# A fused attention and expert block: routing per sequence by ranks and mostly on GpSimd, and a new order of steps

## The reference

```python
def _L0_xattn_ref(image_features, text_features, Wq, bq, Wk, bk, Wv, bv):
    query = einsum('bqi,ih->bqh', image_features, Wq) + bq      # key, value from text_features
    scores = einsum('bqh,bkh->bqk', query, key) * scale
    return einsum('bqk,bkh->bqh', softmax(scores), value)

def _L0_ffn_ref(X, ...):                                        # 16 heads of 8, 8 experts, top 2
    h = rmsnorm(X, norm1_w)
    q, k, v = (h @ w for w in (wq, wk, wv))
    X = X + (softmax(q k^T * scale) v) @ wo
    h2 = rmsnorm(X, norm2_w)
    probs = softmax(h2 @ router_w)
    topw, topi = top_k(probs, 2);  topw = softmax(topw)
    combine = sum(one_hot(topi) * topw)
    shared = swiglu(h2, sh_gate, sh_up, sh_down)
    spec = sum over the 8 experts of combine[:, e] * swiglu(h2, e_gate[e], e_up[e], e_down[e])
    return X + shared + spec

x = x + tanh(g_xattn[0]) * _L0_xattn_ref(_layernorm(x), ctx_768, ...)
x = x + tanh(g_ffn[0]) * _L0_ffn_ref(_layernorm(x), ...)
```

## Time and profile before

| What | Value |
|---|---|
| median of 3 runs | 221.45 us (220.26 to 221.53) |
| profiled execution, device time | 220.48 us |
| its span, first to last instruction | 218.6 us |
| mean granted clock of TensorE | 0.984 |
| busy: PE, DVE, ACT, POOL | 193.9, 139.4, 106.8, 54.6 us |

### The profile page before, as it was taken

One profiled execution on the slowest core, in us unless ns is written; L12 is line 12 of the kernel. 1 busy time (PEld: TensorE's weight loads), 2 busy tenths in 40 slices (PEclk: granted clock), 3 DMA queues, 4 the chain that ended last, 5 costly groups with the idle time before them and its releaser, 6 DMA issues.

```text
span 218.6 us, 4395 instructions
## 1 busy us (share of the span) xinstructions
PE 193.9 (89%) x1575; PEld 167.1 (76%) x1575; DVE 139.4 (64%) x357; ACT 106.8 (49%) x215; POOL 54.6 (25%) x88
## 2 busy tenths in 40 slices
PE   7388995997888979879898989988999999999994
PEld 5265764874866757657686859978999999999993
DVE  2604667789596766857774765889665564554653
ACT  2636374665477757958788734324222223223220
POOL 2917396122010075216841034300000000000000
PEclk9959999999999999999999999999999999999999
DMA  5941993055457935793200000000000000000000
GB/s 139 234 128 22 160 163 42 17 69 69 69 70 94 139 108 70 86 132 103 78 0 0 3 0 0 3 0 1 17 10 3 0 25 3 0 3 24 0 4 24
DMA packets 8998, 11.55 MB, mean 53 GB/s; under 512 B 976, under 2 KB 6992, under 8 KB 8752
## 3 DMA queue, kind: packets, MB, share of 16 engines
q1 hardware_dynamic: 8976, 11.27, 29.1%
HBM read 5.50 MB, written 0.52 MB: 28 GB/s over the span
## 4 chain that ended last, share of the span: by engine, by line
PE 76%; DVE 14%; ACT 4%; issue 3%; POOL 1%; DVEq 0%; POOLq 0%; ACTq 0%
PE bank L1117 14%; PE bank L1106 7%; PE bank L1105 7%; PE bank L1107 7%; PE bank L1088 7%; PE bank L1062 6%; PE bank L1073 5%; DVE mxs L849 4%; PE bank L939 4%; PE bank L954 3%; PE bank L1126 2%; PE bank L930 2%; ACT k_st L519 2%; PE bank L1010 1%; PE bank L946 1%
## 5 line engine op out<-in xcount | busy, mean ns | idle before, releaser
L849 DVE TENSOR_REDUCE mxs<-bank 128x2 f32<-128x512 f32 x64 | 41.4, 687 | 15.2 <-PE bank L1062 14.8
L637 ACT ACTIVATE ep<-bank 128x512 f32<-128x512 f32 x64 | 36.5, 605 | 14.1 <-PE bank L1073 13.6
L1105 PE MATMUL bank<-split,whi 128*128 128x256 f32 x144 | 43.2, 300 | 0.0
L1106 PE MATMUL bank<-split,whi 128*128 128x256 f32 x144 | 40.7, 283 | 0.0
L1107 PE MATMUL bank<-split,wlo 128*128 128x256 f32 x144 | 40.2, 279 | 0.0
L1117 PE MATMUL bank<-down_s,early 128*128 128x128 f32 x288 | 38.3, 276 | 2.1 <-DVE early L866 2.0
L657 ACT ACTIVATE early<-bank 128x512 f32<-128x512 f32 x28 | 16.7, 598 | 46.9 <-PE bank L1107 46.9
L1117 PEld LDWEIGHTS bank<-down_s,early 128*128 128x128 f32 x288 | 35.0, 191 | 2.6 <-DVE early L866 2.2
L869 DVE TENSOR_TENSOR early<-early,bank 128x512 f32<-128x512 f32 x28 | 19.3, 688 | 25.4 <-PE bank L1107 25.3
L1062 PE MATMUL bank<-k_st,q_st 80*128 80x256 f32 x128 | 29.7, 317 | 0.9 <-DVE mxs L849 0.5
L1105 PEld LDWEIGHTS bank<-split,whi 128*128 128x128 f32 x144 | 27.3, 190 | 0.0
(11 more groups left out here) (141 smaller groups left out, 274.2 us busy)
## 6 DMA issues: line engine op xcount, KB each, us to landing
raw<-expert_w SPq DMA_DIRECT2D x9, 256.0 KB, 8.2
k_st<-k_st SPq DMA_DIRECT2D x7, 256.0 KB, 5.8
q_st<-split SPq DMA_DIRECT2D x24, 64.0 KB
k_st<-split SPq DMA_DIRECT2D x24, 64.0 KB
down_s<-expert_w SPq DMA_DIRECT2D x9, 128.0 KB, 8.0
early<-ctx_T SPq DMA_DIRECT2D x1, 672.0 KB, 9.3
xs<-x_tiles SPq DMA_DIRECT2D x2, 256.0 KB, 4.8
out_dram<-x SPq DMA_DIRECT2D x4, 128.0 KB, 1.8
```

The source lines that it names most:

```text
L637: nc.scalar.activation(ep[:, n % NEP].rearrange("p t s -> p (t s)"), b_of(("exp", n))[:], ACT.Exp, scale=SCALE_H).then_inc(free(("exp", n) ...
L849: nc.vector.tensor_reduce(mxs[:, half % 2, :, 64 + h:65 + h], b_of(("max", n))[:].rearrange("p (t s) -> p t s", t=TB), AX_X, ALU.max).then ...
L1105: pe.matmul(bank, whi[:, fs], h2hi[:, hs], start=True, stop=False)
L1106: pe.matmul(bank, whi[:, fs], h2lo[:, hs], start=False, stop=False)
```

## The change

- **Routing.** It is done sequence by sequence. DVE subtracts the largest logit, and compares each logit with each other (128 x 128 results, greater and equal). POOL adds these up to a rank (0 is the largest, ties go to the lower index), and makes the two one-hot tables, the sums, the reciprocals (as powers of -1) and the weights `cw`. Per sequence: 4 instructions on DVE, 7 + 12 + 6 on POOL, 2 on ACT.
- **Moved to POOL.** y = the second layer norm's result (step y, `layer_norm`), the addition of the context to x1 (`add_context`), and the spreading of a half's maxima over 4 rows groups (`spread_maxima`): ACT now writes one group of 256 columns per half, and POOL copies it to the three others. PE waits for that copy (`m_spread`) at every head whose number is 2 modulo 8.
- **Picks.** `copy_picks` is cut in two steps, r0 and r1, which stand further back in ACT's list.
- **Items** go sequence by sequence. DVE waits for `x_ready` and, but for the shared expert, `cw_ready` of the sequence before it adds.
- **Order.** All tables of steps are new. 22 items are placed by i0 (behind slots 56, 60, 70, 71, 75, 79, 80, 81, 101, ...), where 8 were (behind slots 74, 75, 100, ...). k2 moves from slot 12 to 8, m1 and m2 from 11 and 14 to 16 and 25.

```diff
-FIRST_STEPS = """f0 g0 xn0 f1 t0 f2 q0 s0 g1 s1 p0 xn1 z0 g2 xn2 p1 q1 o0 o1 s2 s3 f3 q2 p2 j0 p3 n0 s4 o2 h0 o3
-                 p4 k0 n1 g3 e0 xn3""".split()
+FIRST_STEPS = """f0 f1 g0 f2 xn0 q0 g1 s0 t0 s1 g2 p0 p1 f3 z0 r0 o0 xn1 xn2 o1 q1 s2 s3 y0 j0 q2 p2 g3 p3 n0 r1
+                 h0 o2 s4 o3 k0 n1 p4 e0 h1 w0""".split()
...
-    dense = [(0, 0), (0, 1)] + [(e, b) for b in range(2) for e in range(1, NEXP)]
-    dense += [(e, b) for b in range(2, NB) for e in range(NEXP)]
+    dense = [(e, b) for b in range(NB) for e in range(NEXP)]
...
+            def layer_norm(b):
+                for i in range(b * TB, (b + 1) * TB):
+                    last = nc.gpsimd.tensor_scalar(y[:, i, :], x1[:, i, :], mv[:, 1, i, 0:1], small[:, 5, i:i + 1],
+                                                   ALU.subtract, ALU.mult)
+                last.then_inc(y_ready, 1)
+                pool.wait_ge(y_ready, b + 1)
+
+            def add_context(b):
+                ts = slice(b * TB, (b + 1) * TB)
+                xb, yb = (t[:, ts, :].rearrange("p t d -> p (t d)") for t in (x1, y))
+                hb = xs[:, ts, :].rearrange("p t d -> p (t d)")
+                step(nc.gpsimd.tensor_tensor(hb, yb, tg[:, 1:2].broadcast_to([P, TB * D]), ALU.mult))
+                nc.gpsimd.tensor_tensor(xb, xb, hb, ALU.add).then_inc(x_ready, 1)
+                pool.wait_ge(x_ready, b + 1)
...
+                if kind == "router":
+
+                    pool.wait_ge(rank_in, b + 1)
+                    step(nc.gpsimd.tensor_tensor(alike[:], alike[:], front[:].unsqueeze(1).broadcast_to([P, TB, NE, NE]),
+                                                 ALU.mult))
+                    step(nc.gpsimd.tensor_tensor(more[:], more[:], alike[:], ALU.add))
+                    step(nc.gpsimd.tensor_tensor(alike[:, :, :, 0:4], more[:, :, :, 0:4], more[:, :, :, 4:8], ALU.add))
+                    step(nc.gpsimd.tensor_tensor(more[:, :, :, 0:2], alike[:, :, :, 0:2], alike[:, :, :, 2:4], ALU.add))
+                    nc.gpsimd.tensor_tensor(rank.unsqueeze(3), more[:, :, :, 0:1], more[:, :, :, 1:2],
+                                            ALU.add).then_inc(rank_out, 1)
+                    pool.wait_ge(rank_out, b + 1)
+                    step(nc.gpsimd.tensor_scalar(oh1, rank, 0.0, None, ALU.is_equal))
+                    step(nc.gpsimd.tensor_scalar(oh2, rank, 1.0, None, ALU.is_equal))
...
+                if kind == "route_weights":
+                    pool.wait_ge(route_exp, 2 * b + 2)
+                    step(nc.gpsimd.tensor_tensor(rs[:, 9, ts], rs[:, 7, ts], neg_one, ALU.subtract))
+                    step(nc.gpsimd.tensor_tensor(rs[:, 8, ts], rs[:, 9, ts], neg_one, ALU.pow))
...
+            def spread_maxima(b, half):
+                is_read(pool, ("mT", b, half))
+                rows = q_st[NROW:NSEL, b % NSTACK]
+                nc.gpsimd.tensor_copy(rows[:, 4 * half + 1:4 * half + 4, :],
+                                      rows[:, 4 * half:4 * half + 1, :].broadcast_to([NH, NG // 2 - 1, L])
+                                      ).then_inc(m_spread, 1)
+                pool.wait_ge(m_spread, 2 * b + half + 1)
...
-                    rows = b_of(use)[64:NSEL, 0:L].unsqueeze(1).broadcast_to([NH, NG // 2, L])
-                    nc.scalar.mul(q_st[64:NSEL, b % NSTACK, 4 * half:4 * half + 4, :], rows, -1.0).then_inc(free(use), 1)
+                    nc.scalar.mul(q_st[NROW:NSEL, b % NSTACK, 4 * half, :], b_of(use)[NROW:NSEL, 0:L], -1.0
+                                  ).then_inc(free(use), 1)
...
-                for k, dst, signal in ((6, xs, hs_ready), (5, y, y_ready)):
-                    for i in range(b * TB, (b + 1) * TB):
...
-                    xb = x1[:, ts, :].rearrange("p t d -> p (t d)")
-                    step(nc.vector.scalar_tensor_tensor(out=xb, in0=yb, scalar=tg[:, 1:2], in1=xb,
-                                                        op0=ALU.mult, op1=ALU.add))
...
+                    step(nc.vector.tensor_reduce(rs[:, 0, ts], lg, AX_X, ALU.max))
+                    d1 = rt[:, 0, ts, :]
+                    nc.vector.tensor_tensor(d1, lg, rs[:, 0, ts].unsqueeze(2).broadcast_to([P, TB, NE]),
+                                            ALU.subtract).then_inc(free(("router", b)), 1)
+                    is_read(dve, ("router", b))
+                    mine, other = d1.unsqueeze(3).broadcast_to(square), d1.unsqueeze(2).broadcast_to(square)
+                    nc.vector.tensor_tensor(more[:], other, mine, ALU.is_gt)
+                    nc.vector.tensor_tensor(alike[:], other, mine, ALU.is_equal).then_inc(rank_in, 1)
...
+                dve.wait_ge(x_ready, b + 1)
+                if e:
+                    dve.wait_ge(cw_ready, b + 1)
...
+                    if h % 8 == 2:
+                        pe.wait_ge(m_spread, 2 * b + h // 8 + 1)
```

More of the change, by code:

```diff
@@ L89, in flamingo_block @@
     NG = NH // 2
-    NSEL = 64 + NH
-    groups = [range(0, 2), range(2, NB)]
+    NROW = 64
+    NSEL = NROW + NH
     def step_of(text):
@@ L256, in flamingo_block @@
         xn_ready, hs_ready, hi_ready, y_ready = sem("xn_ready"), sem("hs_ready"), sem("hi_ready"), sem("y_ready")
+        x_ready, m_spread, cw_ready = sem("x_ready"), sem("m_spread"), sem("cw_ready")
+        rank_in, rank_out = sem("rank_in"), sem("rank_out")
         nb_ready = sem("nb_ready")
@@ L370, in _ @@
             nc.gpsimd.memset(router_pad[:], 0.0).then_inc(pool_step, 1)
-            for i in range(NE):
-                last = nc.gpsimd.memset(widx[:, i:i + 1], float(NE - i))
-            last.then_inc(pool_step, 1)
+            nc.gpsimd.memset(neg_one, -1.0).then_inc(pool_step, 1)
+            pool.wait_ge(pool_step, done[0] + 2)
             done[0] += 2
@@ L468, in tables @@
                 pool.wait_ge(ld_ffn, 16)
+                step(nc.gpsimd.memset(front[:], 0.0))
+                for i in range(1, NE):
+                    last = nc.gpsimd.memset(front[:, i, 0:i], 1.0)
+                step(last)
                 nc.gpsimd.tensor_copy(router_pad[:, 0:NE], router_s).then_inc(router_ready, 1)
@@ L482, in _ @@
                     norm2(i // TB)
+                elif stage == "y":
+                    layer_norm(i)
                 elif stage == "z":
@@ L500, in _ @@
                             scale_h2(b)
+                            add_context(b)
+                        if kind in ("router", "route_top", "route_weights"):
+                            route(kind, b)
+                        if kind in ("mT0", "mT1"):
+                            spread_maxima(b, int(kind[2]))
                         if kind == "h2T":
@@ L513, in _, with copy_picks @@
             nc.scalar.mul(Wqk_s[:], b_of(("fold", 0))[:, 0:KD], SCALE_X).then_inc(free(("fold", 0)), 1)
-            def copy_picks(s):
-                picks = ident[64:NSEL, 64:64 + NH].rearrange("r (g p) -> r p g", p=2)
-                for p in range(2):
-                    nc.scalar.copy(k_st[64:NSEL, s, p * NG:(p + 1) * NG, :],
-                                   picks[:, p].unsqueeze(2).broadcast_to([NH, NG, L])).then_inc(picks_ready, 1)
+            def copy_picks(p):
+                picks = ident[64:64 + NH, 64:64 + NH].rearrange("r (g p) -> r p g", p=2)
+                nc.scalar.copy(k_st[64:64 + NH, 0, p * NG:(p + 1) * NG, :],
+                               picks[:, p].unsqueeze(2).broadcast_to([NH, NG, L])).then_inc(picks_ready, 1)
             act.wait_ge(ident_ready, 1)
-            copy_picks(0)
             def xn_turned(b):
@@ L671, in _ @@
                     h_turned(i)
+                elif stage == "r":
+                    copy_picks(i)
                 elif stage == "e":
@@ L731, in second_norm @@
                 dve.wait_ge(norm2_out, b + 1)
-                for k, dst, signal in ((6, xs, hs_ready), (5, y, y_ready)):
-                    for i in range(b * TB, (b + 1) * TB):
-                        last = nc.vector.scalar_tensor_tensor(out=dst[:, i, :], in0=x1[:, i, :], scalar=mv[:, 1, i, 0:1],
-                                                              in1=small[:, k, i:i + 1].broadcast_to([P, D]),
-                                                              op0=ALU.subtract, op1=ALU.mult)
-                    last.then_inc(signal, 1)
+                for i in range(b * TB, (b + 1) * TB):
+                    last = nc.vector.scalar_tensor_tensor(out=xs[:, i, :], in0=x1[:, i, :], scalar=mv[:, 1, i, 0:1],
+                                                          in1=small[:, 6, i:i + 1].broadcast_to([P, D]),
+                                                          op0=ALU.subtract, op1=ALU.mult)
+                last.then_inc(hs_ready, 1)
             def x_max(i):
```

100 lines of the change are left out of this document (42 added, 58 removed), and 27 rows, old and new, of tables (MIXED_STEPS, SEQ_STEPS).

## The result

The changed kernel takes 223.29 us (median of 11 runs, 220.85 to 227.07) against 220.67 us for the kernel before on the same chips: ratio 1.0119, 95% interval 1.0082 to 1.0156. The forecast was 213.7, in a range of 208.5 to 219.5. The profiled execution took 221.48 us, its span is 219.7.

A forecast was written before the change was run, and what follows sets the result against it. PE was taken to bound the kernel, with about 42 us of holes ahead of 149.4, and the DMA chain to set slot 48. 3.8 + 4.0 = 7.8 us off 220.48 gives 212.7, plus 1.0 for the median: 213.7, range 208.5 to 219.5.

The forecast's parts named there:

- The start: Up to slot 0: late picks save 3.7 us, the clock 2.8, y on POOL costs 1.2; 5.3 us earlier.
- From slot 0 to slot 48: The DMA chain sets this stretch, DVE and ACT savings do not count; slot 48 comes 3.8 us earlier, at 94.2.
- the term for the pads: Ahead of slot 48: pads copied later make the stacks' transfers queue, costing 1.5 us of lead (0 to 3.5).
- port contention: POOL holds two-input DVE instructions behind slot 0: DVE loses 14 us, PE perhaps 5; 218.5; chance 0.09, including POOL stalls.
- Behind slot 48: From slot 48 to the end, 120.5 us before: three holes can close, less shifted PE work; 4.0 us gained.
- (2): Behind slot 48: PE's wait for L866, DVE's 15 small routing instructions between two items, goes; 2.1 us gained.
- The 0.9 us of shifted work: About 0.9 us of PE work moves from ahead of slot 48 to behind it, a loss there.
- (3): Tail of sequence 3: of PE's waits of about 1.9 us, 0.3 is gained.
- (1): Ahead of the last heads: five items begin there instead of two, filling 2.5 of PE's 5.4 us to spare.
- POOL: POOL's additions, priced from its nearest rows, raise it from 54.6 to about 101 us, hidden; 0 lost, up to 1.5.
- The slower rival: Behind slot 48: POOL's small instructions at 0.726 us each make PE stand, some 12 us lost; 225; chance 0.05.

The follow-up runs named there:

- the splits apart: Changed kernel with GpSimd's splits of experts 0 and 1 moved (slot 5 to 3, slot 16 to 14), not directly behind second-norm powers: 213.32 us, ratio 0.9694.

## Why the prediction was wrong

*The start* held: 5.6 us of lead at slot 0 against 5.3 forecast, ACT's picks gone from the first tile, clock 1.00 from 10.6 to 17.4.

*From slot 0 to slot 48* is the step that failed. I said that the DMA chain sets this stretch, so that nothing else in it counts, and gave slot 48 a lead of 3.8 us. Measured, it came 0.85 us late. The chain only sets it as long as PE keeps up. PE was held for 2.35 and 2.56 us and then ran at half clock for two stretches of 6.9 us. The runs price that at 9.4 us: 3.1 for the waits, 6.3 for the clock (1.6 of these behind slot 48, see below). With the splits apart, slot 48 lies 60.6 us behind slot 0 (61.3 before) at 91.6, a lead of 6.5 us. So the term for the pads, 1.5 us, was not needed either. From the first DMA of stack 1 to slot 48 it was 56.5 us (35.14 to 91.59), as before, but the DMA share is 0.00 from 90 to 92 us: the DMAs were done at least 1.6 us ahead, and the chain did not set slot 48 there either.

The rival "port contention" had the mechanism, its row (1.371 us) and the rule of the Trainium skill, and still came out at 218.5 with 0.09 for its whole case. It failed in two ways. I spread 14 us of holds evenly over DVE and let a third reach PE. Of the 16 instructions that I placed behind slot 0, four of xs stand ahead of it (20.8 to 29.5 us), and the eight comparisons were not held (281 to 292 ns). The four that are left were all held, by 3.0 us together, and all of it reached PE. The order of POOL's list decides instead: m0 moved from slot 1 to slot 5 (which my list of changes did not name) and m1 from 11 to 16, right behind the two powers that release xs, with DVE and PE both waiting at that moment. The new list laid beside the trace would have shown the danger. And I counted a wait of PE at its own length. The kernel before had shown in the earlier trace rows that PE's standing still costs clock afterwards; I used that for a gain and not for a loss. The evidence against, that the eight steps of y showed no hold, said only that no split met them.

*Behind slot 48* I counted 4.0 us; the changed kernel took 120.8 us there against 120.5. With the splits apart it took 119.2, so 1.3 gained. By its terms: (2) the wait for L866 went, 2.1 us, right. The 0.9 us of shifted work, right: ten small matmuls more stand there (23, 6 and 6 at L1061, L1069 and L1054, against 16, 4 and 5 of their kind before), an estimate of 1.0 us at the 0.1 us from one to the next in a group of L1061. (3) 0.3: nothing. (1) 2.5 us of filled holes: nothing. From slot 48 to the last head's scores it takes 34.1 us for 314 matmuls, against 26.8 for 248. The 66 more cost 7.3 us, where an item's pitch (2.31 us for 20) makes them 7.6. So the holes are nearly what they were. The items do fill some, but those that the change itself makes: without them PE waits for POOL's h and for the spread, and 7.1 us are lost, the slow clock among it. The remaining 1.6 us of the changed kernel fit the slow stretch at 148.0 to 151.4, 3.4 us at half clock. It comes in some kernels and not in others with the same waits of 0.8 and 0.7 us ahead of it; why stays open.

*POOL* was priced well in sum: y 0.88 us each (0.609 forecast, too low), the spread 0.82 (0.85), context 0.61 and 0.73 (0.726), powers of two columns 0.71 to 0.75, small instructions 0.19 to 0.27 up to 32 columns, 0.32 for 64 and 0.46 for 128. The slower rival, small instructions at 0.6, did not occur. With 7.8 us off the span forecast and 7.8 measured (218.6 to 210.8) once the splits are apart, the sum was near by luck: a lead of 6.5 in place of 3.8 at slot 48 made up for 1.3 in place of 4.0 behind it.

## What to carry to other kernels

Work moved within GpSimd's list is not free because GpSimd is idle: look at what DVE does in that very moment, above all right behind a GpSimd instruction that releases DVE, and at which form that instruction has. A wait of PE in mid-kernel is to be priced with the slow clock that may follow, here some 3 us on top of each 1.5 us of hold; if it can't be removed, matmuls on zeros in front of it gave back two thirds of the loss here. Two orders that differ in two splits, each moved by two slots, lay 9 us apart here, so an order should be tried with the suspected pair apart before a change is judged.
